# A 12-block decoder: the last norm and the division's last product of causal attention on other engines, and the context sum's constant terms in wide products

## The reference

```
x = layernorm(x + block(x))          # (x - mean) / sqrt(var + 1e-5)
```

```
a = where(causal, clip(q @ k.T * scale, -100, 100), -inf)
e = exp(a - max(a));  p = e / (sum(e) + 1e-6)
p = p + 1e-8;         p = p / sum(p)
out = (p @ v) @ w_proj.T
```

```
out = concat(x, mean(ctx)) @ W.T + b    # = x @ W1.T + (mean(ctx) @ W2.T + b)
```

## Time and profile before

| | us |
|---|---|
| median of 3 runs | 1964.57 |
| lowest and highest run | 1953.8, 1969.59 |
| the profiled execution | 1968.41 |
| its span, first to last instruction | 1966.6 |

### The profile page before, as it was taken

The page is one execution under the profiler, slowest core; times in us unless marked ns, Lnnn a source line. Parts: engine busy times, 40 slices in busy tenths (PEclk is TensorE's granted clock), DMA queues, the critical chain, the costliest instruction groups (busy, mean ns, idle before and its releaser), DMA issues. The chain is left out here.

```text
span 1966.6 us, 32291 instructions
## 1 busy us (share of the span) xinstructions
PE 1597.7 (81%) x11350; PEld 962.7 (49%) x11389; DVE 1318.9 (67%) x3088; ACT 1047.1 (53%) x1980; POOL 445.7 (23%) x656
## 2 busy tenths in 40 slices
PE   5779957888778999985879999996489888798693
PEld 3546632322465666663634444443255444466572
DVE  4546667778494677664756767785689999575533
ACT  3336636778523444546445555554357666465464
POOL 1110021111124666642200000000210110100475
PEclk8999967889889999997999999997599999798797
DMA  4100021211056888861000000001121120001213
GB/s 122 43 1 2 1 76 54 62 57 54 1 173 252 315 327 325 326 244 44 1 1 1 1 1 1 1 1 41 53 77 44 55 66 12 1 2 35 81 52 90
DMA packets 73337, 152.14 MB, mean 77 GB/s; under 512 B 9810, under 2 KB 57211, under 8 KB 68091
## 3 DMA queue, kind: packets, MB, share of 16 engines
q1 hardware_dynamic: 62571, 136.91, 20.4%
q0 software_dynamic: 4992, 10.23, 1.7%
q10 hardware_dynamic: 5616, 2.94, 0.6%
HBM read 125.51 MB, written 29.26 MB: 79 GB/s over the span
## 5 line engine op out<-in xcount | busy, mean ns | idle before, releaser
L843 DVE TENSOR_REDUCE l1aM<-PS 128x2 f32<-128x1024 f32 x128 | 150.6, 1219 | 37.3 <-PE PS L645 37.0
L165 POOL TENSOR_SCALAR rstd<-MV 128x2 f32<-128x2 f32 (+1 forms) x84 | 20.9, 249 | 601.8 <-DVE MV L133 597.1
L786 ACT ACTIVATE l1aE<-PS 128x1024 f32<-128x1024 f32 x128 | 125.7, 1026 | 26.9 <-PE PS L669 25.4
L2757 ACT COPY PT<-PS 128x512 f32<-128x512 f32 x128 | 69.0, 590 | 86.1 <-PE PS L2658 85.8
L843 DVE TENSOR_REDUCE l3aM<-PS 128x2 f32<-128x256 f32 (+3 forms) x128 | 102.0, 819 | 13.0 <-PE PS L647 10.5
L2879 DVE TENSOR_REDUCE M<-PS 128x1 f32<-128x589 f32 x128 | 92.4, 763 | 22.8 <-PE PS L2647 22.5
L2763 ACT ACTIVATE E<-PS,M 128x589 f32<-128x589 f32 x128 | 95.7, 760 | 22.4 <-DVE M L2879 22.2
L1860 PE MATMUL PS<-WB,H 128*128 128x512 f32 x234 | 107.4, 595 | 0.0
L856 DVE SCALAR_TENSOR_TENSOR l3aE<-l3aE,l3aLB 128x2048 f32<-128x2048 f32 (+1 forms) x64 | 96.3, 1528 | 1.5 <-ACT l3aE L786 1.5
L2001 ACT ACTIVATE H<-PS,WB 128x128 f32<-128x128 f32 x156 | 44.5, 368 | 93.2 <-PE PS L1848 93.2
L786 ACT ACTIVATE l3aE<-PS 128x512 f32<-128x512 f32 (+3 forms) x128 | 82.1, 709 | 13.3 <-PE PS L671 13.2
(11 more groups left out here) (693 smaller groups left out, 4269.9 us busy)
## 6 DMA issues: line engine op xcount, KB each, us to landing
WB<-in_experts SPq DMA_DIRECT2D x39, 1286.0 KB
TB<-mixed_tails SPq DMA_DIRECT2D x39, 768.5 KB, 7.2
head_image<-l1aparts SPq DMA_DIRECT2D x48, 128.0 KB, 2.4
head_image<-l3aparts SPq DMA_DIRECT2D x45, 128.0 KB, 2.4
l1aQS<-head_image SPq DMA_DIRECT2D x16, 256.0 KB, 3.6
l1aKS<-head_image SPq DMA_DIRECT2D x16, 256.0 KB, 4.1
l3aQS<-head_image SPq DMA_DIRECT2D x16, 256.0 KB, 2.9
l3aKS<-head_image SPq DMA_DIRECT2D x32, 128.0 KB, 3.0
```

The source lines that it names most:

```text
L786: nc.scalar.activation(E[:, at:at + 2, q0:S], PS[:, bank:bank + 2, q0:S], ACT.Exp, scale=SCALE).then_inc(exp_done, 1)
L843: v.tensor_reduce(M[:, m % 2, qt, 2 * hp:2 * hp + 2], PS[:, bank:bank + 2, 0:kc], AX, ALU.max, negate=True).then_inc(pair_free, 1)
L2757: nc.scalar.copy(PT[:, n % 2, par, 0:NT, qt * P:(qt + 1) * P], PS[:, slot(x) + 2 * par, :].rearrange("p (t q) -> p t q", t=NT)).then_inc(p ...
```

## The change

In causal attention, and there alone, VectorE's F ends with the sum L874, which now raises a new semaphore `summed_up`; GpSimd waits for it and makes the product into R, raising `ctx_done`. VectorE waits for the product of the group before ahead of the two sums that overwrite its inputs. In the same stage, and in the context sum, `norm_gpsimd` and `norm_apply` give way to `shift_gpsimd` and `shift_scalar`: in causal attention ScalarE does its part at unit Y. In the context sum the products with W2 and with the bias are made once for a batch, over 512 columns (the weight or bias repeated four times), ahead of the four products with W1, which add to them.

```
--- before.py
+++ after.py
@@ -514,11 +514,12 @@
     for i, u in enumerate([u for u in order if u[0] == "V"]):
         freed.update({(u[1], u[2] + n): i + 1 for n in range(u[3])})
     clips = {u[1:]: i + 1 for i, u in enumerate([u for u in order if u[0] == "X"])}
+    g_of = lambda m: m % G
     place = lambda m, kt: HG * ((m * NT + kt) % SETS)
 
     def body(block, projected, high_made, rest_made, middle_made, low_made, zeroed, v_taken, pair_ready, pair_free, max_split, max_turned, max_added, s_ready, exp_done,
              clipped, pool_steps, pv_done, o_copied, o_turned, ctx_done, c_turned, c_taken, out_ready, steps, normed, turned, v_summed, v_added, xt_made,
-             q_imaged, k_imaged, *stacked):
+             q_imaged, k_imaged, summed_up, *stacked):
         parts, left, QS, KS = first.parts, first.left, first.QS, first.KS
         Va = k.sb(name + "Va", [P, 2, NT, H, 32])
         M = k.sb(name + "M", [P, 2, NT, HG])
@@ -751,7 +752,12 @@
                     split_maxima(pool, g, step, m)
                     pool.wait_ge(max_split, m + 1)
                 elif kind == "W":
-                    k.norm_gpsimd(pool, m, m)
+                    (k.shift_gpsimd if causal else k.norm_gpsimd)(pool, m, m)
+                elif kind == "F" and causal:
+                    b = m // G
+                    pool.wait_ge(summed_up, m + 1)
+                    c = k.R[:, b, :, g_of(m) * HG * DK:(g_of(m) + 1) * HG * DK].rearrange("p t (j d) -> p t j d", d=DK)
+                    g.tensor_tensor(c, tt[:, :, :, :], rec[:, :, :].unsqueeze(3).broadcast_to([P, NT, HG, DK]), ALU.mult).then_inc(ctx_done, 1)
 
         @block.scalar
         def _(act):
@@ -795,6 +801,8 @@
                     if m >= 2:
                         act.wait_ge(o_turned, m - 1)
                     nc.scalar.copy(Os[:, m % 2, :], PS[:, 6, :]).then_inc(o_copied, 1)
+                elif kind == "Y" and causal:
+                    k.shift_scalar(act, normed, m, m)
                 elif kind == "C":
                     b = u[1]
                     act.wait_ge(c_turned, b + 1)
@@ -865,28 +873,30 @@
                     c = k.R[:, b, :, g * HG * DK:(g + 1) * HG * DK].rearrange("p t (j d) -> p t j d", d=DK)
                     if causal:
                         svg = sv[:, b % 2, g * HG * DK:(g + 1) * HG * DK].rearrange("p (j d) -> p j d", d=DK).unsqueeze(1)
+                        if m:
+                            dve.wait_ge(ctx_done, m)
                         step(v.tensor_scalar(aa[:, :, :], total, 1e-6, None, ALU.add))
                         step(v.tensor_scalar(rec[:, :, :], total, 1.0 + S * 1e-8, S * 1e-14, ALU.mult, ALU.add))
                         step.wait()
                         step(v.tensor_tensor(tt[:, :, :, :], spread_d(aa[:, :, :]), svg.broadcast_to([P, NT, HG, DK]), ALU.mult))
                         step(v.reciprocal(rec[:, :, :], rec[:, :, :]))
                         step.wait()
-                        step(v.tensor_tensor(tt[:, :, :, :], o, tt[:, :, :, :], ALU.add))
-                        o = tt[:, :, :, :]
+                        v.tensor_tensor(tt[:, :, :, :], o, tt[:, :, :, :], ALU.add).then_inc(summed_up, 1)
                     else:
                         step(v.reciprocal(rec[:, :, :], total))
-                    step.wait()
-                    v.tensor_tensor(c, o, spread_d(rec[:, :, :]), ALU.mult).then_inc(ctx_done, 1)
+                        step.wait()
+                        v.tensor_tensor(c, o, spread_d(rec[:, :, :]), ALU.mult).then_inc(ctx_done, 1)
                 elif kind == "W":
                     b = u[1]
                     dve.wait_ge(out_ready, b + 1)
                     k.norm_stats(dve, PS[:, bank_of[u], :].rearrange("p (t d) -> p t d", t=NT), step, b)
                 elif kind == "Y":
-                    k.norm_apply(dve, normed, u[1], u[1])
+                    if not causal:
+                        k.norm_apply(dve, normed, u[1], u[1])
 
     k.stage(name, ["projected", "high_made", "rest_made", "middle_made", "low_made", "zeroed", "v_taken", "pair_ready", "pair_free", "max_split", "max_turned", "max_added",
                    "s_ready", "exp_done", "clipped", "pool_steps", "pv_done", "o_copied", "o_turned", "ctx_done", "c_turned", "c_taken", "out_ready", "steps",
-                   "normed", "turned", "v_summed", "v_added", "xt_made", "q_imaged", "k_imaged"] + [f"stacked{i}" for i in range(G)], body)
+                   "normed", "turned", "v_summed", "v_added", "xt_made", "q_imaged", "k_imaged", "summed_up"] + [f"stacked{i}" for i in range(G)], body)
 
 
 CROSS = (
@@ -1615,17 +1625,22 @@
             mm = nc.tensor.matmul
             pe.wait_ge(w["landed"], 16)
             for b in range(BT):
+                whole = PS[:, 4 + b, :].rearrange("p (t d) -> p t d", t=NT)
+                mm(whole, cr[:, b, :], w["w2"].unsqueeze(1).broadcast_to([P, NT, P]), start=True, stop=False, skip_group_check=True)
+                mm(whole, k.ones_b, k.bias["l1x_b"].unsqueeze(1).broadcast_to([P, NT, P]), start=False, stop=False, skip_group_check=True)
                 for t in range(NT):
-                    o = PS[:, 4 + b, t * P:(t + 1) * P]
-                    mm(o, k.xt(b)[:, t * P:(t + 1) * P], w["w1"], start=True, stop=False)
-                    mm(o, cr[:, b, :], w["w2"], start=False, stop=False)
-                    ins = mm(o, k.ones_b, k.bias["l1x_b"], start=False, stop=True)
+                    ins = mm(whole[:, t, :], k.xt(b)[:, t * P:(t + 1) * P], w["w1"], start=False, stop=True, skip_group_check=True)
                 ins.then_inc(out_ready, 1)
 
         @block.gpsimd
         def _(pool):
             for b in range(BT):
-                k.norm_gpsimd(pool, b, b)
+                k.shift_gpsimd(pool, b, b)
+
+        @block.scalar
+        def _(act):
+            for b in range(BT):
+                k.shift_scalar(act, normed, b, b)
 
         @block.vector
         def _(dve):
@@ -1634,9 +1649,6 @@
             for b in range(BT):
                 dve.wait_ge(out_ready, b + 1)
                 k.norm_stats(dve, PS[:, 4 + b, :].rearrange("p (t d) -> p t d", t=NT), step, b)
-                if b:
-                    k.norm_apply(dve, normed, b - 1, b - 1)
-            k.norm_apply(dve, normed, BT - 1, BT - 1)
 
     k.stage("l1x", ["out_ready", "steps", "normed"], body)
```

6 lines of the change are left out of this document (2 added, 4 removed).

## The result

The kernel after takes 1976.08 us (median of 21 runs, 1966.11 to 1984.26), the kernel before on the same chip 1968.46 (21 runs, 1953.8 to 1976.9): 1.0041 times as long, 95% interval 1.0025 to 1.0058. The medians differ by +7.6 us where I forecast +2.0, and 1976.08 lies outside my range of 1955 to 1975. Of the 9.6 us to my 1966.5, 3.9 are not of the change: before's median of three runs was 1964.57, that of 21 is 1968.46. The ratio lies within the 1% that I called no change.

What follows compares the result with a forecast made beforehand. VectorE's 97% was taken as no bound: VectorE, TensorE and ScalarE tie in each group's loop. +0.25 - 0.8 + 1.7 + 1.9 - 1.1 = +2.0 us on 1964.57 gave 1966.5 us, range 1955 to 1975.

Steps and rivals of the forecast that it cites:

- part 1: Causal attention: the division's last product moves to GpSimd 16 times; waits covered except in the last group, +0.25 us.
- a plain group doesn't get faster: Causal groups 1 to 14: VectorE's saved 0.32 us becomes a wait for TensorE; 0 gained, last clip to first stays 5.37 us.
- The rival in which VectorE sets the pace: Causal attention: TensorE and ScalarE move up with VectorE, -3.9 us in all, 1960.7 us; chance 0.2.
- the product's size: Causal attention: the moved product takes 0.45 us on GpSimd.
- Its tail term: Last causal group: the transposition waits uncovered for the product on GpSimd, +0.25 us (-0.0 to +1.05).
- batches 0 and 1: Causal norm on ScalarE: VectorE's relief outweighs ScalarE's later copy, -0.4 us each, -0.8 together (-1.5 to +1.4).
- batch 2: Causal norm, last but one group: ScalarE's queue is the path and its copy comes later, +1.7 us (+1.2 to +2.1).
- the tail: Causal norm of the last batch, nothing beside it: the GpSimd and ScalarE chain takes longer, +1.9 us (+1.7 to +2.1).
- the context sum: Context sum's stage with wide products and ScalarE's norm together: -1.1 us (-1.5 to -0.3).
- Part 3: Context sum's products: wide form saves weight loads, 3.85 us instead of 4.3 for the first batch; batch 1 some 0.7 us earlier.
- The rival in which the wide products save nothing: Context sum: only TensorE's columns count, so the stage gains just 0.5 us; +2.6 us in all, 1967.2 us; chance 0.15.
- The rival on the slower side: Causal batches 0 and 1: GpSimd's power holds the shared port and stops clips, +5.0 us in all, 1969.6 us; chance 0.15.

Runs made afterwards that it cites:

- Experiment 1: Kernel before, no operation changed; GpSimd only waits for VectorE's F of the group before, ahead of the key's second subtraction: 1972.76 us against 1966.29, ratio 1.0025.
- experiment 2: Kernel after with the key's second subtraction moved ahead of the product in GpSimd's queue: 1967.09 us against before's 1966.29, ratio 1.0017.
- experiment 4: Kernel before with F's product on GpSimd and the key's second subtraction ahead of it in the queue: 1967.34 us against 1967.78, ratio 1.0002.
- experiment 3: Kernel before with only F's product moved to GpSimd, at the queue place it has in after: 1977.19 us, ratio 1.0036 to before.
- experiment 5: Kernel before with only causal attention's norm applied by ScalarE, GpSimd making the shift: 1972.47 us, ratio 1.0042 to before.
- experiments 7 and 8: Kernel before with one context-sum edit each: wide products alone, stage 17.6 us; ScalarE's norm alone, 18.0 us; before 18.6.
- experiment 9: Kernel before with GpSimd's queue reordered in groups 1, 5, 9: both subtractions first, sums of values held behind the last clip; 1961.12 us against 1967.78, ratio 0.9965.

## Why the prediction was wrong

**The step that failed** is the end of part 1: "Who waits for it ... All covered." I listed who waits for the product, and never what is queued behind its wait on GpSimd. The new wait went into a queue whose next instruction, in groups 1, 5 and 9, was the key's second subtraction. It cost 10.07 us in groups 2, 6 and 10 and gave 2.6 back in 1, 5 and 9. Part of the cost is TensorE's idle time for the late transfer, and part the half clock that came with it: at 1.6 us for 3.4, the 10.3 us at 0.50 in groups 2 and 6 make nearly half of the 10.07 (an estimate). Experiment 1 makes the loss without the product, experiment 2 takes it away with the product kept. The code shows the order of the units, and the earlier trace rows show GpSimd busy just there; both were at hand.

**Right: a plain group doesn't get faster.** 5.37 us from last clip to first, as before, with a wait of 0.43 us where the product was. The rival in which VectorE sets the pace falls, in after and in experiment 4: 97% busy and no bound.

**Right: the product's size**, 0.41 us for my 0.45. Its tail term, +0.25, came as +0.17 and -0.07 in experiments 3 and 4, which can't be told from nothing.

**Right alone, wrong in company: batches 0 and 1.** Forecast -0.4 each, -0.32 twice in experiment 5 and for batch 0 in experiment 2, but +0.26 in after. There the late transfer kept TensorE, so ScalarE's copies for unit T end only at 1546.20, 0.05 us behind the last clip (1544.34 + 1.81 = 1546.15), and Y begins then. In experiment 5 Y began 0.5 us ahead of the last clip's end (1548.70 against 1549.21). The same four activations thus push the copy of Os 0.58 us further (1.74 us behind the last clip instead of 1.16), and VectorE waits for it: ahead of the reduction 1.03 us where experiment 2 has 0.85, and 0.31 at the sums where experiment 2 has nothing. The failed step cost 1.2 us here too (twice 6.38 - 5.80).

**Right in its mechanism, small in size: batch 2.** +2.29 for +1.7, at the place forecast: the chain's first two instructions took 1.09 and 0.66 us among the clips, the copy stands right behind Y at 1674.08, the clip waits 2.12 us for ScalarE. In experiment 2 it was +1.71: there ScalarE runs from that copy to the clip without a wait, with the granted clock at 1.00 for the first 5.0 of the 7.66 us. In after, where the clock was 0.50 from 1669.3 to 1679.5, ScalarE waits 0.32 us for TensorE once more. Before's 5.94 isn't free of the clock either: with the full one it is 5.03 (experiment 3), and against that the term is +2.6 (7.66 - 5.03).

**Right: the tail.** From the end of L133 to the end of the norm 3.55 us (1697.83 - 1694.28), before 1.81: +1.74 for +1.9.

**Right in sum, wrong in its parts: the context sum.** -0.9 for -1.1. I gave the wide products 0.7 and the norm 0.4 of it; the norm measures 0.56 and the wide products 0.37 (experiments 7 and 8). Part 3 of the prediction has batch 1 some 0.7 us earlier, and that is the term that was mis-sized here; the products of the first batch take 3.97 us (from 526.75 to the next wide pair at 530.72) for my 3.85. The rival in which the wide products save nothing falls too.

**The rival on the slower side** named the wrong mechanism. The power stops no clip (experiment 5). It came nearest in its time, for a reason that wasn't its own: luck. On the Trainium skill's rule, GPSIMD Engine Reference, section 1 (Specifications), that GpSimd and VectorE contend for shared SBUF interfaces: the runs agree for GpSimd's long instructions, on both sides. I had used it for the clips alone; the casts and subtractions of 128x16 elements are hit as well, and that is where a gain lay that the change didn't look for.

Added up: 2.0 forecast, +7.45 for the queue (10.07 - 2.62), +1.3 in batches 0 and 1, +0.6 in batch 2, -0.2 in the tail and +0.2 in the context sum make 11.4; less the 1.1 us of the profiled execution that is 10.3, and the two stages measured 10.98 - 0.85 = 10.1. The medians say +7.6, and the ratio's interval +4.9 to +11.4.

## What to carry to other kernels

When an operation goes to an idle engine, write down that engine's queue as a list and look at what stands behind the new wait: an engine that is busy 23% of the time still has instructions that are due, and here one of them fed a DMA on which TensorE waited in three groups. Then ask what the idle engine's long instructions already do to the busy one; moving those by a few microseconds was worth 7.7 us, more than any part of the change gained. When two profiles have equal spans, compare them stage by stage before you believe it. And when the same group takes half a microsecond or more longer in one profile than in another, read TensorE's granted clock over that stretch first.

## What the runs showed of the hardware

GpSimd instructions of 128x512 elements and these VectorE instructions with SBUF operands alone ran one behind the other, whichever came second: a clip of 1536 columns 2.72 us instead of 1.75, a cast of 128x16 elements 1.11 instead of 0.21, a subtraction of 128x16 1.06 instead of 0.18 us, and GpSimd's subtraction 2.21 instead of 1.15 behind a clip. The waiting instruction shows it as its own duration, not as idle time. The clamp of the maxima (L546, 128x16) is no such case: 0.18 us beside the last 0.15 us of a GpSimd sum, 0.16 in experiment 9 with nothing beside it. VectorE's reductions out of PSUM kept their time beside GpSimd's sums (three in 2.91 us at 1472.43 in experiment 9, as in the group behind without them at 1480.32 in after). GpSimd's power of 1.04 us over 128x4 elements held no clip.

TensorE's granted clock fell from 1.00 to 0.50 in seven of the nine places where TensorE had idled 2.7 to 4.0 us for the late transfer, during that wait or just behind it. Such 3.4 us at 0.50 cost 1.6 us in group 6; where no transfer was late, they cost 0.76 ahead of group 2 (before) and 0.58 ahead of group 11 (experiment 9).
